# A causal attention block with two heads side by side: column tiles of 64, a causal edge of 64 and a new order on every engine

## The reference

```python
y = _layernorm(x, ln_w, ln_b)
q = jnp.einsum('bsd,hde->bhse', y, wq)       # 16 heads of 8
k = jnp.einsum('bsd,hde->bhse', y, wk)
v = jnp.einsum('bsd,hde->bhse', y, wv)
scores = jnp.einsum('bhse,bhte->bhst', q, k) / math.sqrt(HEAD)
scores = scores + causal                     # -inf above the diagonal
weights = jax.nn.softmax(scores, axis=-1)
attn = jnp.einsum('bhst,bhte->bshe', weights, v).reshape(...)
x = _layernorm(x + (attn @ wo + x))
x = _layernorm(x + (x @ W.T + b + x @ lilora_weight.T))
```

## Time and profile before

| | us |
|---|---|
| median of 3 runs | 441.14 (440.78 to 442.62) |
| span of the profiled execution | 438.9 |
| PE busy | 418.9 (95%) |
| DVE busy | 381.2 (87%) |
| ACT busy | 342.3 (78%) |
| POOL busy | 307.2 (70%) |
| mean share of the DMA engines in queue 1 | 58.0% |

### The profile page before, as it was taken

How to read it: one execution, slowest core, us unless ns; L and a number is a source line. 1 busy time by engine, 2 the same in 40 slices (tenths; PEclk the granted TensorE clock), 3 DMA queues, 4 the chain that set the end, 5 groups by cost and what they waited for, 6 DMA issues and landing times.

```text
span 438.9 us, 15728 instructions
## 1 busy us (share of the span) xinstructions
PE 418.9 (95%) x5571; PEld 335.4 (76%) x5571; DVE 381.2 (87%) x1056; ACT 342.3 (78%) x865; POOL 307.2 (70%) x395
## 2 busy tenths in 40 slices
PE   7698999999999999999999999999999999999994
PEld 3356677878888877888888888888888888878762
DVE  5589888989899989999999999999999999989664
ACT  2376778778888887888888888888888888888871
POOL 7854857767677786777777787777777778754763
PEclk9699999999999999999999999999999999999998
DMA  2656566556666656667667656665776665664111
GB/s 75 163 161 170 151 155 174 152 158 166 185 188 170 174 158 162 172 171 192 185 167 181 179 161 183 166 172 162 190 193 171 182 167 147 163 169 137 50 40 38
DMA packets 77866, 69.13 MB, mean 158 GB/s; under 512 B 9291, under 2 KB 68482, under 8 KB 77826
## 3 DMA queue, kind: packets, MB, share of 16 engines
q1 hardware_dynamic: 76398, 67.67, 58.0%
q10 hardware_dynamic: 1428, 0.95, 0.8%
HBM read 47.07 MB, written 20.99 MB: 155 GB/s over the span
## 4 chain that ended last, share of the span: by engine, by line
PE 75%; DMA 9%; SPq 7%; DVE 5%; issue 2%; ACT 1%; POOL 0%; ACTq 0%; POOLq 0%; DVEq 0%
PE pv_bank L1356 18%; PE score_bank L1337 11%; PE bank L1369 10%; PE bank L1364 7%; PE max_bank L1323 6%; PE max_bank L1324 5%; PE max_bank L1319 5%; PE score_bank L1338 5%; PE bank L1426 3%; PE bank L1427 3%; DMA xr<-in_x 2%; DMA xa<-in_x 2%; DVE rowmax L1035 2%; DMA kx<-k_rows 2%; SPq L292 2%
## 5 line engine op out<-in xcount | busy, mean ns | idle before, releaser
L1035 DVE TENSOR_REDUCE rowmax<-max_bank 128x2 f32<-128x512 f32 (+1 forms) x384 | 245.7, 675 | 15.5 <-PE max_bank L1324 8.5
L608 ACT ACTIVATE probs<-score_bank 128x384 f32<-128x384 f32 x512 | 222.1, 491 | 39.5 <-PE score_bank L1338 27.2
L505 POOL TENSOR_SCALAR_AFFINE_SELECT probs<-probs 128x1024 f32<-128x1024 f32 x127 | 137.5, 1093 | 59.6 <-ACT probs L608 59.4
L1337 PE MATMUL score_bank<-qx,kx 74*128 74x256 bf16 x512 | 119.8, 273 | 0.8 <-DMA qx<-mT 0.8
L1338 PE MATMUL score_bank<-qx,kx 74*128 74x128 bf16 x512 | 101.6, 218 | 0.0
L1356 PE MATMUL pv_bank<-probs,v_ext 128*32 128x256 f32 x2032 | 97.5, 329 | 0.0
L1323 PE MATMUL max_bank<-kx,qx 128*128 128x128 bf16 x512 | 86.6, 221 | 2.9 <-DVE rowmax L1035 2.8
L1324 PE MATMUL max_bank<-kx,qx 74*128 74x128 bf16 x512 | 86.2, 220 | 0.0
L1356 PEld LDWEIGHTS pv_bank<-probs,v_ext 128*32 128x32 f32 x2032 | 56.3, 109 | 31.9 <-issue 6.8
L1323 PEld LDWEIGHTS max_bank<-kx,qx 128*128 128x128 bf16 x512 | 48.5, 98 | 16.2 <-DVE rowmax L1035 6.1
L1337 PEld LDWEIGHTS score_bank<-qx,kx 74*128 74x128 bf16 x512 | 49.7, 97 | 6.6 <-issue 1.6
(11 more groups left out here) (123 smaller groups left out, 606.5 us busy)
## 6 DMA issues: line engine op xcount, KB each, us to landing
kx<-k_rows SPq DMA_DIRECT2D x187, 96.0 KB
qx<-q_rows SPq DMA_DIRECT2D x128, 96.0 KB
qx<-q_rows SPq DMA_DIRECT2D x64, 104.0 KB
q_rows<-parts SPq DMA_DIRECT2D x32, 192.0 KB, 2.1
k_rows<-parts SPq DMA_DIRECT2D x31, 192.0 KB, 2.4
xa<-in_x SPq DMA_DIRECT2D x32, 128.0 KB, 3.5
xr<-in_x SPq DMA_DIRECT2D x32, 128.0 KB, 2.2
out<-y SPq DMA_DIRECT2D x32, 128.0 KB, 3.1
```

Source lines behind the costliest of these rows:

```text
L505: pool.affine_select(out=t, in_=t, compare_op=ALU.is_ge, fill=0.0, base=0, pattern=[[0, GROUP * NB], [1, P]], channel_multiplier=-1)\
L608: act.activation(probs[:, h, 0:PW], score_bank[SCORE_BANK[h]][:, 0:PW], ACT.Exp, scale=SCALE / Q_SCALE)\
L1035: dve.tensor_reduce(to, of, AX.X, ALU.max).then_inc(s_mread[unit], 1)
L1337: pe.matmul(b[:, 0:SEQ], k[0:SCORE_ROWS, i, 0:P], q[0:SCORE_ROWS, i, :], start=True, stop=True)
```

## The change

Two heads now share a unit. Head `slot(half, 0, p)` writes PSUM partitions 0 to 63 and head `slot(half, 1, p)` partitions 64 to 127, each product having 64 output rows: a block of 64 queries (in `max_scores`) or of 64 keys (in `scores`). Tokens are cut in four blocks of 64 instead of two of 128, so that the causal part is 640 columns per head at 64 rows, where it was 384 at 128 rows. The diagonal block of 64 is masked by 32 mask rows (`DIAGONAL_ROWS` = 106) in both kinds of scores; `mask` on POOL is gone. `exp` runs over 512 columns in 10 units, `row_max` in 11 units, four of which have 384 columns and the others 512. `pv` contracts two heads at once (64 keys of each on the 128 partitions; `v_ext` holds them in separate columns): four quads per half over 256, 192, 128 and 64 columns.

Linear layers, queries and keys, values and the transposition of the maxima are also cut in products of 64 output rows. `load_max_rows` needs four transfers instead of two; `expand` reads two pieces per row. DRAM scratch is doubled (by parity of the batch). `second_parts` and `normalize_f` move from ACT to POOL, the attention transpose goes to `bank6`, and the second norm's statistics are one step later. Every order (`first`, `step`, `last`, on each engine) is new; the end no longer uses spare banks, separate last norms or filler products (`keep_busy`).

```diff
+BLOCK = 64
+BLOCKS = SEQ // BLOCK
...
+DIAGONAL_ROWS = SCORE_ROWS + BLOCK // RUN
...
             def max_scores(it, o, unit):
...
-                if kind == 0:
-                    for g in range(GROUP):
-                        h = quad * GROUP + g
-                        ins = pe.matmul(b[:, g * P:g * P + P], q[:, h, 0:P], k[:, h, 0:P], start=True, stop=True)
-                else:
...
+                width, s = (block + 1) * BLOCK, slice(block * BLOCK, (block + 1) * BLOCK)
+                for n, (g, p) in enumerate(pairs):
+                    at = n * width
+                    if block:
+                        for which in range(2):
+                            h = slot(g, which, p)
+                            pe.matmul(b[which * BLOCK:(which + 1) * BLOCK, at:at + width - BLOCK], q[0:SCORE_ROWS, h, s],
+                                      k[0:SCORE_ROWS, h, 0:width - BLOCK], start=True, stop=True)
+                    for which in range(2):
+                        h = slot(g, which, p)
+                        ins = pe.matmul(b[which * BLOCK:(which + 1) * BLOCK, at + width - BLOCK:at + width], q[0:DIAGONAL_ROWS, h, s],
+                                        k[0:DIAGONAL_ROWS, h, s], start=True, stop=True)
...
-            def scores(it, o, h):
+            def scores(it, o, unit):
...
-                pe.matmul(b[:, 0:SEQ], k[0:SCORE_ROWS, i, 0:P], q[0:SCORE_ROWS, i, :], start=True, stop=True)
-                pe.matmul(b[:, SEQ:PW], k[0:SCORE_ROWS, i, P:SEQ], q[0:SCORE_ROWS, i, P:SEQ],
-                          start=True, stop=True).then_inc(s_score[h], 1)
+                for p, block in [(kind, i) for i in (0, 1, 3)] if kind < PAIRS else [(p, 2) for p in range(PAIRS)]:
...
+                    for which in range(2):
+                        h = slot(half, which, p)
+                        ins = pe.matmul(b[which * BLOCK:(which + 1) * BLOCK, at:at + BLOCK], k[0:DIAGONAL_ROWS, h, t],
+                                        q[0:DIAGONAL_ROWS, h, t], start=True, stop=True)
+                    if block < BLOCKS - 1:
+                        for which in range(2):
+                            h = slot(half, which, p)
+                            ins = pe.matmul(b[which * BLOCK:(which + 1) * BLOCK, at + BLOCK:at + width], k[0:SCORE_ROWS, h, t],
+                                            q[0:SCORE_ROWS, h, (block + 1) * BLOCK:SEQ], start=True, stop=True)
...
             def exp(it, o, h):
-                act.activation(probs[:, h, 0:PW], score_bank[SCORE_BANK[h]][:, 0:PW], ACT.Exp, scale=SCALE / Q_SCALE)\
+                act.activation(probs[:, unit, :], score_bank[SCORE_BANK[unit]][:, :], ACT.Exp, scale=SCALE)\
...
-            def mask(it, o, group):
-                pool.wait_ge(s_exp[GROUP * group + GROUP - 1], it.done(o))
...
+                for block in range(BLOCKS):
+                    for p in range(PAIRS):
+                        unit, at = place(half, p, block)
+                        ins = pe.matmul(pv_bank[VW * p:VW * p + VW, block * BLOCK:SEQ], v_ext[r][:, block, half * PAIRS + p, :],
+                                        probs[:, unit, at:at + SEQ - block * BLOCK], start=block == 0, stop=block == BLOCKS - 1,
...
             def linear(to, source, weight, signal):
                 for n in range(NB):
-                    ins = pe.matmul(to[:, n * D:n * D + D], source[:, n * P:n * P + P], weight[:, :],
-                                    start=True, stop=True)
+                    for c in range(0, P, BLOCK):
+                        ins = pe.matmul(to[c:c + BLOCK, n * D:n * D + D], source[:, n * P + c:n * P + c + BLOCK], weight[:, :],
+                                        start=True, stop=True)
...
             def load_max_rows(it, o):
...
-                for part in range(MAX_PARTS):
-                    sp.dma_start(qx[it.ring(o)][SPLIT_ROWS + part:SPLIT_ROWS + part + 1, :, :],
-                                 mT[part * HEADS:(part + 1) * HEADS, :]).then_inc(s_mrow, 16)
+                n = HALVES * PAIRS * BLOCKS
+                for which in range(2):
+                    for part in range(MAX_PARTS):
+                        at = (which * MAX_PARTS + part) * n
+                        sp.dma_start(qx[it.ring(o)][SPLIT_ROWS + part:SPLIT_ROWS + part + 1, which * HALF:(which + 1) * HALF, :],
+                                     mT[at:at + n, :]).then_inc(s_mrow, 16)
...
+            def second_parts(it, o):
+                pool.wait_ge(s_rest, it.done(o))
...
+                pool.tensor_copy(parts[:, 1, :, :], rest[:, :, :]).then_inc(s_p2, 1)
```

More of the change, by code:

```diff
@@ L35, with last_in_bank, slot, of_half @@
 NORMS = 3
-Q_SCALE = 2.0 ** -72
-RUN = 3
 FIRST_XR = 2
[L45 to L49, removed]
+RUN = 2
+DIAGONAL_ROWS = SCORE_ROWS + BLOCK // RUN
+Q_MASK = [2.0 ** 46, 2.0 ** -31]
+K_MASK = [0.0, -1.0]
+K_AFTER = -(2.0 ** 77)
+MAX_KINDS = 5
+MAX_UNITS = HALVES * MAX_KINDS + 1
+KINDS = PAIRS + 1
+UNITS = HALVES * KINDS
 SCORE_BANKS = 3
[L51 to L57, removed]
+SCORE_BANK = [0, 1, 2] * 3 + [1]
+def last_in_bank(unit):
+    g = unit - 1
+    while SCORE_BANK[g % UNITS] != SCORE_BANK[unit]:
         g -= 1
     return g
-def head(slot):
-    return slot // HALF * HALF + 2 * (slot % GROUP) + slot % HALF // GROUP
+def slot(half, which, pair):
+    return which * HALF + half * PAIRS + pair
+def of_half(heads, half):
+    return heads.rearrange("r (a m) s -> r a m s", a=2)[:, :, half * PAIRS:(half + 1) * PAIRS, :]
+def place(half, pair, block):
+    return (half * KINDS + PAIRS, pair * 2 * BLOCK) if block == 2 else (half * KINDS + pair, {0: 0, 1: SEQ, 3: UNIT - BLOCK}[block])
 class Iteration:
@@ L823, in step @@
+                if it.runs(0):
+                    exp(it, 0, 7)
+                    copy_pv(it, 0, 0)
+                    exp(it, 0, 8)
+                    exp(it, 0, 9)
                 if it.runs(4):
@@ L1263, in last @@
[L1263 to L1273 removed]
+                stats_z(at, 30)
@@ new lines, in max_scores @@
+                if kind == 0 and unit < MAX_UNITS - 1:
+                    pe.wait_ge(s_expand[half], it.done(o, EXPAND))
+                pe.wait_ge(s_mread[(unit - 2) % MAX_UNITS], it.done(o if unit >= 2 else o - 1))
+                b = max_bank[(unit + it.parity(o)) % 2]
+                if unit == MAX_UNITS - 1:
+                    block, pairs = 0, [(g, p) for g in range(HALVES) for p in range(PAIRS)]
+                elif kind == MAX_KINDS - 1:
+                    block, pairs = 1, [(half, p) for p in range(PAIRS)]
+                else:
+                    block, pairs = BLOCKS - 1 - kind // 2, [(half, 2 * (kind % 2)), (half, 2 * (kind % 2) + 1)]
@@ L1345, in pv @@
+                ins.then_inc(s_score[unit], 1)
+            def pv(it, o, half):
+                r = it.ring(o)
+                pe.wait_ge(s_exp[half * KINDS + KINDS - 1], it.done(o))
                 if it.static:
@@ L1636, in step @@
-                if it.runs(0):
-                    scores(it, 0, 11)
+                    bank_free(it, ((s_f, -3),), ((s_norm[1], -2),), ((s_z, -3),), ((s_norm[0], -2),), ((s_vx, 2),))
+                    values(it, 3)
+                if it.runs(1):
+                    max_scores(it, 1, 9)
+                if it.runs(0):
+                    scores(it, 0, 1)
+                if it.runs(1):
+                    max_scores(it, 1, 10)
+                if it.runs(0):
+                    scores(it, 0, 2)
@@ new lines, in step @@
+                if it.runs(0):
+                    scores(it, 0, 5)
+                if it.runs(2):
+                    max_scores(it, 2, 2)
+                if it.runs(0):
+                    scores(it, 0, 6)
+                if it.runs(2):
+                    max_scores(it, 2, 3)
+                if it.runs(0):
+                    scores(it, 0, 7)
+                if it.runs(4):
+                    bank_free(it, ((s_mT, 1),), ((s_aTs, -2),), ((s_rest, 3),), ((s_zTs, -3), (s_yT, 3),))
+                    x_transpose(it, 4)
```

1379 lines of the change are left out of this document (580 added, 799 removed).

## The result

The changed kernel takes 603.27 us (median of four runs, 601.86 to 611.72) where the kernel before, beside it, takes 440.96 (438.44 to 442.62). The ratio is 1.3651, with an interval of 1.3584 to 1.3718. One of the four runs (611.72) is over 1.5% above the fastest, at a lower granted clock, and is left out of the ratio. The prediction said 422, with 405 to 446 as its range: wrong in sign and far outside.

A forecast was written before the change was run, and what follows sets the result against it. TensorE, 95% busy, was taken as the bound: its 12.2 us step falls to 11.1, 11.35 with SP interference. 27 x 0.85 = 23 us saved and 4.5 added give 420.4 from 438.9, stated as 422, range 405 to 446.

The forecast's parts named there:

- The step that failed: SP's twelve expansion issues a step: cutting rows in 2 x 2048 bytes, before one piece of 4096, was priced at nothing.
- Rival (b): SP sets the step, if mT issues take 0.8 each or two-piece rows 0.45: 443 us, or 435 at 12.0; chance 0.21.
- TensorE's sum: TensorE's work per mid-kernel step: 12.2 - 0.8 - 0.43 - 0.25 + 0.4 = 11.1 us.
- Duos: Paired 64-row score products on TensorE: 29, 56 and 83 ns for 64, 128 and 192 columns, saving 0.8 us a step.
- The halves of attention times values: On TensorE, each half as four quads falls from 1.44 to 1.08 us plus entry, saving 0.43 us a step.
- Layout changes: Switches of TensorE's array layout: seven a step instead of four, at 0.13 us each, adding 0.4 us.
- rival (a): Weight loads set small duos on TensorE: 57 ns, not 29, a step of 13.3 us, 475 us in all; chance 0.16.
- DVE, ACT and POOL stay under TensorE: Other engines' work per step: DVE 11.4 to 10.1 us, ACT 10.4 to about 7.5, POOL 9.1 to about 7.5.
- Slack of SP: The sync queue's 1.96 us a step of waiting, mostly for mT, was taken as room for added issues.
- Start and end: Outside the regular steps: +3 us at the start from SP's issues, +1.5 at the end, 4.5 us in all.
- SP was put at 11.1 us a step: Sync queue's work: 10.25 us plus 1.2 for four maxima issues, less some 0.3 for signals and waits that go.
- its 0.25 for SP and TensorE in each other's way: Mid-kernel allowance because SP and TensorE are level at 11.1 us: 0.25 us added, giving a step of 11.35.

The follow-up runs named there:

- the version at 448: The changed kernel with the heads of a half stored contiguously (one-piece expansion rows) and the loop of batches 8 to 27 written out: 448.18 us, ratio 1.0166.

## Why the prediction was wrong

**The step that failed** is this one: "Issues of the expansion keep their count; their rows are cut in 2 x 2048 bytes ... so the number of pieces hardly counts and I take nothing." Measured: 0.755 to 0.86 us for 0.365, twelve times a step (10.2 us for 4.7), so that SP, which waits for nothing, fills a step of 17.5 us. Alone it costs 103 us in the kernel before, and undoing it gives back 128 of 162 here. The proof taken for it was the issue for xr, 0.38 us with 2 x 128 short pieces. That is an issue over 128 partitions; the 24-row issues are charged otherwise, and the price of a row of theirs with two pieces was in no row. Rival (b) had the mechanism, at 0.45 instead of 0.78, and with the right price its own formula gives it: 12 x 0.4 more on 11.1 to 11.4 is 16 a step. Its other condition, 0.8 for an issue of the maxima, came half true: 0.7 in the mean, 2.8 us a step for the 2.4 of the sum. (By its own formula a step of 12.0 gives 440, not 435.) At this one place an unseen operation got one value and no upper end, on the one engine with 0 to 0.3 us left.

**A term that was missing**: the loop body grew (10929 products in place of 5571), and TensorE now stops for 3 to 4 us in each pass of four steps while instructions are fetched. The page before showed the fetched instructions as 23 packets, none of them in the later passes of the loop, and the loop cost nothing there; the prediction did not ask whether twice the instructions would stay. It is worth 27 us once the queue is not the bound, 10 when it is.

**Right, and hidden.** TensorE's sum was 11.1 us a step; the kernel written out with contiguous halves shows 11.4. Duos were put at 29, 56 and 83 ns and step by 32, 59 and 87 in the median of the two gapless steps: with 80, 16 and 16 of them that is 0.35 us more than counted. The halves of attention times values, 1.08 plus a layout change, take 1.23. Layout changes were put at 0.13 and take 0.09: 0.12 from the last duo to attention times values (221.93 to 222.05), of which the duo is 0.03, and 0.32 for two transposes and the way out, where two take 0.23 in the earlier trace rows. By these the seven changes give 0.3 back, so another 0.2 of the 11.4 lies in parts that were not taken apart. So rival (a), duos of 57 ns by their weight loads, is refuted; the page figure of the Trainium skill cited with it (TensorE: Matmul & The Clock Gate, LDWEIGHTS: columns / 1.2 ns, 53 for 64) does not set the pace of duos here, which start 32 ns apart. With the drain at a mode switch that the Trainium skill states (TensorEngine Tiling (Array Packing), Key Properties) the trace agrees: those 0.09 us. DVE, ACT and POOL stay under TensorE as said, at 10.5, 8.7 and 6.2 us a step; the sums were 10.1, 7.5 and 7.5, so ACT came out 1.2 fuller than counted.

**Slack of SP.** "Its waits for mT are slack that it gives back" was a half truth. In the kernel before four issues for two, 1.2 us a step by count and 1.4 measured, cost 38 us, of which 25 came from what stood behind the wait. **Start and end**, put at +4.5, were +24 under the slow queue, and the span less 27 steps is 4.8 more than before in the profile of the version at 448 (start -5, end +10): the sum right, its parts not.

**A third term** stayed hidden under the first: SP was put at 11.1 us a step, and in the version at 448 it works 12.1, of which 1.1 are the long issues behind fetched instructions; without them it would be 11.0, as predicted. With them even contiguous halves and no loop miss the forecast of 422 by 26 us. The trace of before shows such issues where its instructions are still being fetched (ten in the 27 steps, up to 1.8 us), but the prediction took SP's work from 204 to 400 us, where there is one; its 0.25 for SP and TensorE in each other's way was all that it had for them. So the second and the third term have one root: twice as many products are instructions to fetch, and by the packets' times a fetch holds TensorE at the loop and SP all along.

**Open**: why 24 rows of two pieces are charged like two issues when 72 rows of one piece are charged 0.73 and xr's 256 pieces 0.39; whether other orders of the dimensions would keep the 72-row transfers wide; why a fetch holds some issues of SP and not others (29 long ones for 74 packets), and what fewer packets would give, since no version has the new products with fewer of them; whether the last 0.9 us over TensorE's 11.4 are SP's alone; the end, 10 us longer than before in the version at 448.

## What to carry over

When an edit touches an access pattern, price its issues from a row of the same form (rows, pieces, partitions), and where none is there give it twice the price as upper end; on a queue that is within a tenth of the bound this decides the sign. Before a loop body is doubled, look at the fetched instructions in the page, ask what the branch costs when they do not stay, and add up what they take from the queue that issues transfers; read an engine's work from a stretch that fetches as the new kernel will. An engine's waits are room only for work that nothing stands behind: read what is queued after the waiting instruction before you spend them.

## What was not expected of the hardware

- An issue of 24 rows costs 0.365 us with rows of 2048, 4096 or 8192 bytes, and 0.755 to 0.86 with rows in two pieces of 2048.
- Bf16 products of 64 output rows on two column halves of the array start pairwise every 32 ns for 64 columns; they need their columns (0.43 ns each, by the steps of 32 and 87 ns for 64 and 192) and some 4 ns, though each pair has two loads of 64 columns.
- Instructions fetched rise from 0.38 to 1.49 MB for a body of twice the products, with stops of TensorE of 3 to 4 us in each pass of the loop, which end 1.5 to 1.8 us behind a fetched packet; written out, 1.43 MB are fetched and TensorE has no such stop.
- A fetch of instructions holds the queue that issues transfers: issues of 0.9 to 2.2 us, where those of the expansion take 0.365 in the median, end 0.3 to 0.45 us behind a fetched packet (39 of 39 in the kernel before and the version at 448).
- A transfer whose pattern is 3 turns of 24 rows has three packets in flight, one of 24 rows about twelve; a store of one issue and one of two behind such transfers take 1.9 and 8.0 us, where they took 0.4 and 1.1.
